# Token-tile transposes issued in pairs into two PSUM banks, and variance sums as one-column products

## The reference

```
y  = scan(...) + x * D                       # per token, 8 groups of 512 channels
var = mean(yg * yg, axis=-1)                 # one number per token and group
yn = yg * rsqrt(var + 1e-5) * norm_weight * silu(gate)
out = yn @ out_proj_w.T
```

## Time and profile before

| what | value |
|---|---|
| median of three runs | 1660.18 us (1657.32 to 1662.29) |
| the profiled execution: its own time | 1662.89 us |
| its span, first to last instruction | 1661.1 us |
| mean granted TensorE clock | 0.991 of full speed |
| busy share of TensorE, VectorE, ScalarE, GpSimd | 97%, 64%, 52%, 47% |

### The profile page before, as it was taken

One profiled execution on the slowest core, in us unless ns is written; L12 is line 12 of the kernel. 1 busy time (PEld: TensorE's weight loads), 2 busy tenths in 40 slices (PEclk: granted clock), 3 DMA queues, 4 the chain that ended last, 5 costly groups with the idle time before them and its releaser, 6 DMA issues.

```text
span 1661.1 us, 31702 instructions
## 1 busy us (share of the span) xinstructions
PE 1619.4 (97%) x12495; PEld 1300.1 (78%) x12495; DVE 1066.9 (64%) x1772; ACT 857.0 (52%) x1378; POOL 780.9 (47%) x766
## 2 busy tenths in 40 slices
PE   9999999999999999999999999999999999998997
PEld 6678888888888888877778888888888888886665
DVE  6967666566656566777676656665656666564456
ACT  4654546555555555455554555555555545554221
POOL 4464645545463636444254554546364645544103
PEclk9999999999999999999999999999999999999999
DMA  6110102011111111020112201111011102016772
GB/s 202 35 58 29 43 20 64 27 52 39 46 45 33 58 34 43 16 64 26 33 39 71 65 27 52 39 41 50 33 58 33 39 20 65 27 35 148 167 164 102
DMA packets 50291, 93.09 MB, mean 56 GB/s; under 512 B 5664, under 2 KB 6304, under 8 KB 50144
## 3 DMA queue, kind: packets, MB, share of 16 engines
q1 hardware_dynamic: 50144, 91.06, 19.0%
HBM read 82.59 MB, written 8.45 MB: 55 GB/s over the span
## 4 chain that ended last, share of the span: by engine, by line
PE 81%; issue 7%; ACT 4%; POOL 4%; DVE 3%; POOLq 0%; DVEq 0%
PE PS L478 47%; PE PS L744 19%; PE PS L592 3%; PE PS L1084 2%; PE PS L1030 2%; PE PS L650 2%; PE PS L711 2%; ACT big L533 1%; PE PS L357 1%; PE PS L602 1%; PE PS L570 1%; DVE cb L513 1%; POOL yl L704 1%; PE PS L571 1%; PE PS L206 1%
## 5 line engine op out<-in xcount | busy, mean ns | idle before, releaser
L478 PE MATMUL PS<-xh,wh 128*128 128x512 f32 x1280 | 529.7, 414 | 0.6 <-DVE xl L367 0.6
L478 PE MATMUL PS<-xh,wl 128*128 128x512 f32 x1280 | 503.2, 393 | 0.0
L478 PE MATMUL PS<-xl,wh 128*128 128x512 f32 x1280 | 500.3, 391 | 0.0
L513 DVE SCALAR_TENSOR_TENSOR cb<-PS,P,cb 128x496 f32<-128x496 f32 (+2 forms) x576 | 412.6, 716 | 98.4 <-ACT cb L499 82.7
L182 POOL TENSOR_TENSOR wl<-rw,wh 128x512 fp32r<-128x512 f32 x160 | 207.4, 1299 | 183.6 <-ACT wh L177 165.2
L478 PEld LDWEIGHTS PS<-xh,wl 128*128 128x128 f32 x1280 | 240.5, 188 | 55.9
L478 PEld LDWEIGHTS PS<-xh,wh 128*128 128x128 f32 x1280 | 241.1, 188 | 46.2 <-ACT wh L177 1.0
L478 PEld LDWEIGHTS PS<-xl,wh 128*128 128x128 f32 x1280 | 241.9, 189 | 43.1
L698 POOL TENSOR_TENSOR ysum<-yq 128x256 f32<-128x256 f32 x128 | 95.5, 746 | 375.4 <-ACT yq L686 375.4
L499 ACT ACTIVATE cb<-PS,P 128x512 f32<-128x512 f32 x192 | 149.2, 777 | 221.2 <-PE PS L478 220.9
L744 PE MATMUL PS<-oh,yh 128*128 128x512 f32 x512 | 203.0, 396 | 6.4 <-POOL yl L704 5.4
(11 more groups left out here) (193 smaller groups left out, 2238.1 us busy)
## 6 DMA issues: line engine op xcount, KB each, us to landing
rw<-in_w_in SPq DMA_DIRECT2D x160, 256.0 KB, 2.7
ro<-in_w_out SPq DMA_DIRECT2D x64, 256.0 KB, 2.9
wh<-x2s SPq DMA_DIRECT2D x32, 258.5 KB, 5.0
wl<-x2s SPq DMA_DIRECT2D x32, 258.5 KB, 5.2
x2s<-acc SPq DMA_DIRECT2D x16, 260.0 KB, 4.0
out_x<-acc SPq DMA_DIRECT2D x16, 256.0 KB, 2.3
acc<-in_x SPq DMA_DIRECT2D x3, 1024.0 KB, 9.6
acc<-in_x SPq DMA_DIRECT2D x4, 256.0 KB, 4.1
```

The source lines that it names most:

```text
L478: fn = lambda e, k=k, w=w, v=v, i=i: e.matmul(PS[:, bank, :], w[:, m, 128 * k:128 * k + 128], v[:, k, a:a + 512], start=(i == 0), stop=(i ...
L513: dve.op(lambda e, d=d, w=w: e.scalar_tensor_tensor(out=cv[:, :, d:32], in0=pv[:, :, 0:32 - d], scalar=w, in1=cv[:, :, d:32], op0=ALU.mult ...
```

## The change

The transposes of the tiles go to banks `TB` = (2, 5, 2, 7). A(n,0) and A(n,1) are both issued in slot 7 behind seg, and A(n,2) and A(n,3) both in slot 9 ahead of Y(n,0); nothing of them is left in slot 8 and in slot 0 of the next stage. `A_dve(n, 1)` moves from slot 9 to slot 8. The banks are shared with other work, so waits are added: A(n,1) on acc(n-1,2), A(n,3) on L(n,0), Y(n,0) on dtx(n,1), and O(n,0) (bank 7) on dtx(n,3) where it waited on L(n,0). Transposes no longer wait on the dtx just before them.

`S` multiplies `yss` by one column of ones in place of 128. The tiles 1 and 2 of a step are summed behind O(n,2), and their variance and reciprocal root are made by one instruction each on VectorE and GpSimd, in slot 5; `add_out` of tile 1 moves from slot 4 to slot 5 with them. The tiles 0 and 3, and all four of the last step, stay single. `yss` has four buffers, in a part of `big`.

```
+        TB = (PT, PO[2], PT, PO[0])
...
+        def sums(n):
+            return ((0,), (1, 2), (3,)) if n < NS - 1 else ((0,), (1,), (2,), (3,))
...
         def A(n, i):
-            for m in range(6):
-                pe.wait("silu", (n, m))
-            if z >= 1:
-                pe.wait("dtx", divmod(z - 1, 4))
-            if z == 0:
-                pe.wait("alo", 0)
+            if i == 0:
+                for m in range(6):
+                    pe.wait("silu", (n, m))
+                if n >= 1:
+                    pe.wait("dtx", (n - 1, 2))
+                else:
+                    pe.wait("alo", 0)
+            elif i == 1:
+                pe.wait(*(("acc", (n - 1, 2)) if n >= 1 else ("xl", 7)))
+            elif i == 2:
+                pe.wait("dtx", (n, 0))
+            else:
+                pe.wait("L", (n, 0))
...
         def Y(n, i):
             if i == 0:
                 pe.wait("L", (n, 1))
+                pe.wait("dtx", (n, 1))
...
+        def S(n, tiles):
+            last = (n, tiles[-1])
+            pe.wait("ys2", last)
             pe.wait(*shared[0])
-            shared[0] = ("var", (n, i))
-            pe.op(lambda e: e.matmul(PS[:, PG, 256 + 128 * r:384 + 128 * r], yss[:, r, :], C[:, C_ONE:C_ONE + 128],
-                                     start=True, stop=True), "S", (n, i))
+            shared[0] = ("var", last)
+            for i in tiles:
+                fn = lambda e, i=i: e.matmul(PS[:, PG, 256 + i:257 + i], yss[:, i, :], C[:, C_ONE:C_ONE + 1], start=True, stop=True)
+                pe.op(fn, "S", last) if i == tiles[-1] else pe.op(fn)
...
         def O(n, i):
             if i == 0:
-                pe.wait("L", (n, 0))
+                pe.wait("dtx", (n, 3))
...
-                    when = dict(O=(1, 3, 4, 5), rstd=(2, 4, 5, 6), acc=(2, 4, 5, 6)) if real else ...
+                    when = dict(O=(1, 3, 4, 5), acc=(2, 5, 5, 6)) if real else ...
...
                     if m == 8:
                         A_dve(n, 0)
+                        A_dve(n, 1)
                     if m == 9:
                         M_dve(n, 0)
-                        A_dve(n, 1)
                         M_dve(n, 1)
...
                     if m == 7:
                         seg(n)
                         expo(n)
-                    if m >= 7:
-                        A(n, m - 7)
+                        A(n, 0)
+                        A(n, 1)
                     if m == 9:
+                        A(n, 2)
+                        A(n, 3)
                         Y(n, 0)
                         Y(n, 1)
-                if prev and m == 0:
-                    A(n - 1, 3)
```

More of the change, by code:

```diff
@@ L102, in adaln_attn_ffn_kernel @@
         ysum = sb("ysum", [128, 256])
-        yss = sb("yss", [128, 2, 128])
         vr = sb("vr", [128, 4])
@@ L114, in adaln_attn_ffn_kernel @@
         gin_t = y[:, 0, 0:GELU_IN]
+        yss = big[:, 7168:7680].rearrange("p (i t) -> p i t", i=4)
         w4 = sb("w4", [128, 3, 32])
@@ L455, in adaln_attn_ffn_kernel, with summed @@
         shared = [("mx", 3)]
+        def sums(n):
+            return ((0,), (1, 2), (3,)) if n < NS - 1 else ((0,), (1,), (2,), (3,))
+        def summed(n, i):
+            return next(g[-1] for g in sums(n) if i in g)
         def who(n):
@@ L581, in A @@
         def A(n, i):
-            z, a = 4 * n + i, 128 * i
+            a = 128 * i
             if i == 0 and n in block_at:
                 pe.wait("dre", (block_at[n], 1))
-            for m in range(6):
-                pe.wait("silu", (n, m))
-            if z >= 1:
-                pe.wait("dtx", divmod(z - 1, 4))
-            if z == 0:
-                pe.wait("alo", 0)
+            if i == 0:
[11 more added lines that the diff above has]
+                pe.wait("L", (n, 0))
             for j in range(4):
-                fn = lambda e, j=j: e.transpose(PS[:, PT, 128 * j:128 * j + 128], xs[:, j, a:a + 128], ident)
+                fn = lambda e, j=j: e.transpose(PS[:, TB[i], 128 * j:128 * j + 128], xs[:, j, a:a + 128], ident)
                 pe.op(fn, "T", (n, i)) if j == 3 else pe.op(fn)
@@ L622, in A_dve @@
             dve.op(lambda e: e.tensor_tensor(
-                dtx[:, r, :].rearrange("p (h c) -> p h c", h=8), PS[:, PT, :].rearrange("p (h c) -> p h c", h=8),
+                dtx[:, r, :].rearrange("p (h c) -> p h c", h=8), PS[:, TB[i], :].rearrange("p (h c) -> p h c", h=8),
                 bc(dtt[:, 4 * tb + i, 8 * g:8 * g + 8].rearrange("p (h o) -> p h o", o=1), 128, 8, 64), ALU.mult), "dtx", (n, i))
@@ L699, in y_pool @@
             pool.wait("ys1", (n, i))
-            if z >= 2:
-                pool.wait("S", divmod(z - 2, 4))
-            pool.op(lambda e: e.tensor_tensor(yss[:, r, :], ysum[:, 0:128], ysum[:, 128:256], ALU.add), "ys2", (n, i))
+            if n >= 1:
+                pool.wait("S", (n - 1, summed(n - 1, i)))
+            pool.op(lambda e: e.tensor_tensor(yss[:, i, :], ysum[:, 0:128], ysum[:, 128:256], ALU.add), "ys2", (n, i))
             pool.wait("yh", (n, i))
             pool.op(lambda e: e.tensor_tensor(yl[:, r, :], yg[:, :], f(yh[:, r, :]), ALU.subtract), "yl", (n, i))
-        def S(n, i):
-            z, r = 4 * n + i, i % 2
-            pe.wait("ys2", (n, i))
+        def S(n, tiles):
+            last = (n, tiles[-1])
+            pe.wait("ys2", last)
@@ L722, in rstd_pool, with rstd @@
-        def rstd_pool(n, i):
-            z = 4 * n + i
-            pool.wait("var", (n, i))
+            shared[0] = ("var", last)
+            for i in tiles:
+                fn = lambda e, i=i: e.matmul(PS[:, PG, 256 + i:257 + i], yss[:, i, :], C[:, C_ONE:C_ONE + 1], start=True, stop=True)
+                pe.op(fn, "S", last) if i == tiles[-1] else pe.op(fn)
+        def rstd(n, tiles):
+            a, b, last = tiles[0], tiles[-1] + 1, (n, tiles[-1])
+            dve.wait("S", last)
+            if n >= 1:
+                dve.wait("rs", (n - 1, summed(n - 1, tiles[-1])))
+            dve.op(lambda e: e.tensor_scalar(vr[:, a:b], PS[:, PG, 256 + a:256 + b], 1.0 / 512.0, 1e-5, ALU.mult, ALU.add), "var", last)
+            pool.wait("var", last)
@@ L725, in rstd_pool @@
             pool.wait("mh", 0)
-            if z >= 4:
-                pool.wait("acc", divmod(z - 4, 4))
-            pool.op(lambda e: e.tensor_tensor(rs[:, i:i + 1], vr[:, i:i + 1], mh[:, 0:1], ALU.pow), "rs", (n, i))
+            if n >= 1:
+                pool.wait("acc", (n - 1, tiles[-1]))
+            pool.op(lambda e: e.tensor_tensor(rs[:, a:b], vr[:, a:b], bc(mh[:, 0:1], 128, b - a), ALU.pow), "rs", last)
         def O(n, i):
@@ L752, in add_out @@
             dve.wait("O", (n, i))
-            dve.wait("rs", (n, i))
+            dve.wait("rs", (n, summed(n, i)))
             dve.wait("X", T)
@@ L818, in stage @@
                 if prev:
-                    when = dict(O=(1, 3, 4, 5), rstd=(2, 4, 5, 6), acc=(2, 4, 5, 6)) if real else dict(O=(1, 2, 3, 4), rstd=(2, 3, 4, 5),
-                                                                                                   acc=(2, 3, 4, 5))
+                    when = dict(O=(1, 3, 4, 5), acc=(2, 5, 5, 6)) if real else dict(O=(1, 2, 3, 4), acc=(2, 3, 4, 5))
                     at = lambda kind: [i for i in range(4) if when[kind][i] == m]
-                    for i in at("rstd"):
-                        rstd_dve(n - 1, i)
-                        rstd_pool(n - 1, i)
+                    for tiles in sums(n - 1):
+                        if when["acc"][tiles[-1]] == m:
+                            rstd(n - 1, tiles)
                     for i in {0: (0,), 1: (1,), 3: (2, 3)}.get(m, ()):
@@ L902, in stage @@
                         O(n - 1, i)
-                        S(n - 1, i)
+                        for tiles in sums(n - 1):
+                            if tiles[-1] == i:
+                                S(n - 1, tiles)
                 if real:
```

## The result

The changed kernel takes 1757.72 us (median of 4 runs, 1753.27 to 1758.87) against 1661.24 us of the kernel before (median of 4 runs): a ratio of 1.0579, 95% interval 1.0551 to 1.0606. The profiled execution has a span of 1757.1 us and a mean granted clock of 0.980, against 1661.1 us and 0.991.

The account below looks back on a forecast made before the run. TensorE, 97% busy and back to back in the stages, was taken as the bound. 1662.9 + 74.6 + 2.8 + 1 - 0.8 + 24 = 1764.5 us, forecast 1762 as that execution is 2.7 us above the median; range 1725 to 1796.

Parts of the forecast that it names:

- The new wait: O(n-1,0) waits on VectorE's dtx(n-1,3): 2.44 us in 28 stages, 2.1 in three, 74.6 us in all.
- the slide of 0.43: Slot 9 holds one more group of transposes, so proj(n,0) and its chain come 0.43 us later while O's place stays.
- TensorE's own work: Variance products and grouped transposes on TensorE: saving 0; only the loop's transpose waits on dtx go, 0.8 us gained.
- The variance products: 128 products in S: one column saves 0, bounds 0 and 28 us; rival cheap product with the wait, 1734 us, chance 0.10.
- The clock: Half-speed stretches after about half the new spells, 24 us; rivals: behind all 53 us, chance 0.17; behind none, 0.17.
- DT_pe: In slot 5 of stages 1, 16 and 17 it may wait for the later acc of tile 1: 1 us, bounds 0 to 3.
- The last stage: O(31,0) waits for dtx of tile 3, which follows yg of tile 1: its start slides by 2.8 us.
- (1): Profile sign: TensorE waits for O on VectorE's dtx about 31 times, 2.2 to 2.3 us idle each, 70 us in all.
- (2): Profile sign: from a single variance product's start to the second matmul behind it, still 0.45 us.
- (3): Profile sign: idle time of transposes before dtx gone, and groups of eight transposes 0.86 us long.
- (5): Profile sign: VectorE's taps, y, yg and dtx of slot 1 as close together as now.
- (4): Profile sign: granted clock lower than 0.991, about 0.96 from 14 more stretches.

Follow-up runs that it names:

- experiment 1: Changed kernel with dtx of tile 3 made in slot 0, behind M of tile 2 and ahead of the taps of proj(n,0): 1659.65 us, ratio 0.9991.
- alone (2): Kernel before with one wait added, O(n,0) also waiting on dtx(n,3): 1736.0 us, ratio 1.0444.
- halved (4): Changed kernel with dtx of tile 3 ahead of y and yg of tile 1, behind the taps, in slot 1: 1695.44 us, ratio 1.0207.
- 5 to 8: Kernel before, variance product as one column: 1658.25 us; five times with one column: 1764.83; with 128: 1770.63; one column, four of five loading 32: 1721.31.
- run 3: Changed kernel with nine matmuls of 512 columns, result unread, filling the spell between proj(n,1) and O(n-1,0): 1736.99 us, ratio 1.0463.
- experiment 9: experiment 1 plus silu of projection 1 ahead of evac of projection 2, and single sums in steps 0, 15 and 16: 1647.53 us, ratio 0.991.

## Why the prediction was right

It forecast 1762 us and 1757.7 were measured; the mechanism, its place and its count are as forecast. That the number is so close is in part luck, by two errors that cancel and a guess on the clock.

- *The new wait.* Forecast 2.44 us in each of 28 stages. Measured 2.82 - 0.23 = 2.59 (2.43 of it idle). dtx was done 1180.17 - 1177.73 = 2.44 us after TensorE could have come to O, where the earlier trace rows and the slide of 0.43 gave 2.38; from its end to O are 0.15 us where 0.06 were taken. In stages 1 and 17 the idle time is 2.64 us and not shorter than elsewhere, as the prediction had it (2.1). Undone (1), alone (2) and halved (4), the wait moves the time the way that it must if it is the cause.
- *TensorE's own work.* Forecast 0, with 0.8 us for the wait of transposes. The net stage is 2.45 us longer and the wait is 2.59, so TensorE's work is 0.14 us a stage shorter, 31 x 0.14 = 4 us; with the wait gone (1) a stage is 0.23 us shorter than before, 7 us. This term was put at nothing and is the one that was mis-sized. The prediction looked at the product and one matmul behind it, and the difference lies further on: in the trace of before the twelve matmuls behind four transposes take 1114.03 - 1111.18 = 2.85 us and the twelve behind a variance product 105.44 - 102.58 = 2.86, against 102.44 - 99.72 = 2.72 for twelve of O behind a projection. The change leaves fewer such places in a stage. The 4 us cancelled in the sum the 31 x 0.15 = 4.7 us by which the wait was taken too short.
- *The variance products.* Right: the load of 128 columns sets the pace (5 to 8), and of the two sections of the Trainium skill's page "TensorE: Matmul & The Clock Gate" it is "LDWEIGHTS (loading the stationary operand)", which spoke against a saving, that the runs bear out: 0.21 us for two loads of 128 columns, and 0.032 us from start to start with 32. The gap of 25 ns a pass, from the table of "Back-to-back issue gap", would have given 21 us, and fails in the run of one column (about 2 us) and of five of one column (0.21 us each). The prediction said that the two sections disagree, and they do not: the second gives its table for products taken alone, and says that in a stream of loads and products both set the spacing.
- *The clock.* Forecast 14 additional stretches and 24 us; there were 12 and 20 us. The number was a choice between 0 and 31, so its nearness is luck; that they cost, run 3 shows. The spell of 1.41 us in stage 0 that "brought none" was followed by a stretch at half speed in the changed kernel (the spell ends at 38.52, the stretch begins at 38.62), so it was no sign that the place decides.
- *DT_pe.* Forecast 1 us, bounds 0 to 3. In the changed kernel 1.4 us. With the large wait gone (1) it is 4.2 us, above the bound, so the large wait covers part of it in the changed kernel.
- *The last stage.* Forecast +2.8 us. From the transposes of tile 2 to O of tile 0 were 1521.51 - 1515.36 = 6.15 us, and are 1618.14 - 1609.05 = 9.09: +2.9.
- *What the profile after would show.* (1) 31 spells of 2.43 us of idle time where 2.2 to 2.3 were said, and under the name of ScalarE's yh where VectorE's dtx was said; (2), (3) and (5) as said; (4) 0.980 and not 0.96, where 14 stretches were turned into a mean wrongly: 12 stretches of 3.4 us at half speed are 1.2% of the span.

## What to carry to other kernels

A buffer that is borrowed for a short time comes free when its reader's queue gets to it, not when the data are ready: before a bank is shared, find the reader's place in its engine's written order and compare its end with the start of the next writer. Here one line moved on VectorE turns a loss of 96 us into nothing. Between 1 and 128 moving columns, a product with 128 loaded columns costs its load, so fewer moving columns save next to nothing; whether the reduction is cheaper with the two operands exchanged was not tried. When a wait is taken away, look at what it had covered: in experiment 9 the time moved to the next two waits. And where the profile names a releaser for a wait on several semaphores, check that the named instruction is of the tile that is waited for.

## What the runs showed of the hardware

- How often the clock fell rose with the length of the idle spell, with dense work on both sides and 31 spells in the profiled execution of each run: 0.39 us none, 1.10 us none, 1.94 us four, 2.43 us twelve. Length and surroundings do not decide alone: of the two spells of 1.67 us before the mixing products both were followed by it in experiment 1, one in the changed kernel and none in experiments 3 and 4. What decides was not found.
- 128 moving columns against one: 0.216 and 0.208 us a product of two passes. 32 loaded columns against 128: 0.032 and 0.112 us from one pass to the next, and about 0.3 us a group at its edges.
- Eight transposes in a row and the projection behind them are cheaper than two groups of four with a projection behind each. The timeline of the kernel after has

```profile
1259.55 1.03 PE L607 MATMUL PS<-C,big 128*128 128x128 f32 x8
1260.34 0.48 PE L486 MATMUL PS<-xh,wh 128*128 128x512 f32 x1
1260.65 0.39 PE L486 MATMUL PS<-xl,wh 128*128 128x512 f32 x1
```

and from the start to the second matmul are 1.10 us, 0.86 for the eight, as two groups at 0.43; the gain is only in the matmuls further on (2.72 against 2.85 us, above), and what slows those behind a change of kind was not tried.
